# Conditioned residual on one core: loads and stores of the turns cut at other places, and one wait of the store queue taken out

## What is computed

```python
w = weights[conditions]                                # (64, 64, 64) out of (200, 64, 64)
return x + jnp.einsum('bct,bcd->bdt', x, w)            # x is (64, 64, 512)
```

## Time and profile before

| | |
|---|---|
| median of three executions | 46.13 us (45.98 to 49.01) |
| the profiled execution | 45.98 us, span 44.7 us in the trace |
| TensorE busy | 30.7 us, 69% of the span |
| VectorE busy | 15.1 us, 34% |
| ScalarE busy | 13.4 us, 30% |
| DMA | 17.83 MB, 399 GB/s over the span |
| mean granted clock of TensorE | 0.992 of full speed |

### The profile page before, as it was taken

The page is one execution under the profiler, slowest core; times in us unless marked ns, Lnnn a source line. Parts: engine busy times, 40 slices in busy tenths (PEclk is TensorE's granted clock), DMA queues, the critical chain, the costliest instruction groups (busy, mean ns, idle before and its releaser), DMA issues.

```text
span 44.7 us, 329 instructions
## 1 busy us (share of the span) xinstructions
PE 30.7 (69%) x100; PEld 13.2 (29%) x100; DVE 15.1 (34%) x24; ACT 13.4 (30%) x16; POOL 1.6 (4%) x9
## 2 busy tenths in 40 slices
PE   0040000699999679999999799999999999910000
PEld 0040000435334045452543244534445344200000
DVE  1310000000019980957820580094095082073000
ACT  0894000000000072935800580093094080071000
POOL 4009000000000000000000000000000000000000
PEclk9999999999999999999999999999999999999996
DMA  0589999999999999999997988998899999999993
GB/s 0 88 337 403 433 425 411 455 418 418 455 403 447 499 440 469 469 469 469 469 440 315 418 374 374 528 484 352 381 396 425 455 381 403 433 440 396 418 425 139
DMA packets 1586, 17.83 MB, mean 399 GB/s; under 512 B 178, under 2 KB 178, under 8 KB 178
## 3 DMA queue, kind: packets, MB, share of 16 engines
q1 hardware_dynamic: 1440, 16.78, 89.2%
q0 software_dynamic: 144, 1.05, 5.6%
q10 hardware_dynamic: 2, 0.00, 0.0%
HBM read 9.44 MB, written 8.39 MB: 399 GB/s over the span
## 4 chain that ended last, share of the span: by engine, by line
DMA 50%; PE 31%; SPq 4%; DVE 3%; issue 1%; POOLq 0%
DMA x_sb<-x 50%; PE product L166 31%; SPq L94 4%; DVE y_sb L216 3%; POOLq L134 0%
## 5 line engine op out<-in xcount | busy, mean ns | idle before, releaser
L166 PE MATMUL product<-x_sb,w_diag 128*128 (+1 forms) x40 | 17.7, 597 | 0.3 <-POOLq L134 0.3
L216 DVE COPY y_sb<-product 128x1024 f32<-128x1024 f32 x8 | 9.8, 1225 | 12.8 <-PE product L166 10.5
L117 ACT COPY y_sb<-product 128x1024 f32<-128x1024 f32 x8 | 8.1, 1013 | 13.6 <-PE product L166 11.3
L146 PE MATMUL product<-x_sb 128*128 128x512 f32 x10 | 7.0, 872 | 5.3 <-DMA x_sb<-x 5.3
L166 PEld LDWEIGHTS product<-x_sb,w_diag 128*128 128x128 f32 x40 | 7.4, 190 | 10.5 <-issue 10.5
L158 PE MATMUL product<-x_sb,w_all 64*64 64x512 f32 x48 | 5.5, 599 | 0.7 <-DVE w_all L205 0.7
L146 PEld LDWEIGHTS product<-x_sb 128*128 128x128 f32 x10 | 2.8, 288 | 8.8 <-issue 8.8
L111 ACT COPY w_diag<-w_all 64x256 f32<-64x256 f32 x1 | 0.6, 628 | 12.1 <-DVE w_all L205 12.1
L202 DVE TENSOR_TENSOR gathered<-gathered,piece 128x64 f32<-128x64 f32 x1 | 0.3, 270 | 10.1 <-DMA gathered<-weights,table_row 10.1
L158 PEld LDWEIGHTS product<-x_sb,w_all 64*64 64x64 f32 x48 | 2.5, 199 | 3.6 <-issue 2.2
L205 DVE STREAM_TRANSPOSE w_all<-gathered 128x2048 f32<-128x2048 f32 x1 | 2.3, 2312 | 0.0
(11 more groups left out here) (9 smaller groups left out, 1.3 us busy)
## 6 DMA issues: line engine op xcount, KB each, us to landing
x_sb<-x SPq DMA_DIRECT2D x4, 1024.0 KB, 9.1
x_sb<-x SPq DMA_DIRECT2D x1, 4096.0 KB, 22.3
out<-y_sb SPq DMA_DIRECT2D x1, 3072.0 KB, 9.7
out<-y_sb SPq DMA_DIRECT2D x3, 1024.0 KB, 5.0
out<-y_sb SPq DMA_DIRECT2D x1, 2048.0 KB, 6.9
condition<-conditions ACTq DMA_DIRECT2D x1, 0.2 KB
gathered<-weights,table_row POOLq DMA_INDIRECT x1, 9.7
```

The source lines that it names most:

```text
L117: nc.scalar.copy(y_sb[:, 4 * turn:4 * turn + 2, :], product[turn % SETS][0][:, :, :]).then_inc(moved_by_act, 1)
L146: nc.tensor.matmul(product[1][0][:, 0, :], x_sb[:, 0, 0:P], x_sb[:, 0, :], start=True, stop=True)
L166: product_of = nc.tensor.matmul(product[s][j][:, g, :], w_diag[:, s, 2 * j + g, :], x_pair(2 * j + g), start=True, stop=True)
L216: nc.vector.tensor_copy(y_sb[:, 4 * turn + 2:4 * turn + 4, :], product[turn % SETS][1][:, :, :]).then_inc(moved_by_dve, 1)
```

## The change

`LOADS` had one load for turns 4 to 7 (4 MB); now turn 4 is loaded by itself (1 MB) and turns 5 to 7 together (3 MB). `STORES` had turns 0 to 2 in one store (3 MB), turns 3 and 4 in one (2 MB), then single turns; now turns 0 and 1 are one store, turns 2 and 3 one (2 MB each), and turns 4 to 7 are stored singly. The wait ahead of the first store is taken out.

```diff
-    LOADS = [(0, 0), (1, 1), (2, 2), (3, 3), (4, 7)]
-    STORES = [(0, 2), (3, 4), (5, 5), (6, 6), (7, 7)]
+    LOADS = [(0, 0), (1, 1), (2, 2), (3, 3), (4, 4), (5, 7)]
+    STORES = [(0, 1), (2, 3), (4, 4), (5, 5), (6, 6), (7, 7)]
...
-
-            sp.wait_ge(moved_by_dve, SETS + 1)
             for first, last in STORES:
```

## The result

The changed kernel takes 47.10 us (median of 6, 46.75 to 47.17), the kernel before 46.07 us (median of 6). The ratio is **1.022, 95% interval 1.020 to 1.024**: slower by about 1.0 us. The forecast was 46.1, no change, with a range up to 46.7. One of the six executions before, at 49.01 us, fell in a slower state of the chip and is left out of the ratio. The profiled execution took 46.75 us (span 45.4 us), the quickest of its six and 0.77 us more than the profiled one of before, so the trace shows some three quarters of the loss.

What follows compares the result with a forecast made beforehand. The prediction took the DMA engines as the bound: 45.98 us profiled, + 0.1 for packets, - 0.05 for the two starts, gives 46.03; with the median 0.15 above the profiled execution, it forecast 46.1 us, no change, range 45.6 to 46.7.

Steps and rivals of the forecast that it cites:

- The bound: Whole kernel: the DMA engines limit it, at 2.4 to 2.5 us per MB; TensorE's chain is a close second.
- The chain's rival: TensorE's turns 4 to 7: their 0.32 to 0.90 us gain reaches the end, 45.1 to 45.7 us; chance 0.09.
- The wait's removal: Ahead of the first store: alone gives 0; with the new list the store is issued 1.8 us sooner, gaining 0 to 0.05.
- A store that stands in the queue sooner starts no sooner: First store, behind the loads: earlier issue doesn't start its data earlier, as loads last until about 25.1; gain 0 to 0.05 us.
- The signs that I had named: 3 MB load landing after 26, or steps above 2.6 us per MB, would mean reads and writes hinder each other.
- The row I leaned on: Old kernel's 4 MB load: kept 2.42 us per MB with the first store queued for its last 2.36 us.
- The rival of the shared queue: Early store alternates with the 3 MB load, which lands near 29.2, delaying turn 5; 46.6 to 47.4 us; chance 0.08.
- Packets and further transfers: Loads and stores cut into more, smaller transfers: 0.02 to 0.21 us more, taken as 0.1.
- The uncovered part of a transfer: Two further transfers: each shows up to 2.35 us that are not data, giving 47 to 50.7 us; chance 0.03.

Runs made afterwards that it cites:

- multiplied3: The changed kernel with the first store held until TensorE is through with turn 2; 46.82 us, ratio 1.017 to the kernel before.
- hold_landed: The changed kernel with the first store held until the 3 MB load has landed; 47.72 us, ratio 1.040 to the kernel before.

## Why the prediction was wrong

**The bound** was named rightly. The DMA engines set the end, and TensorE's chain does not: TensorE lost its stop before turn 4, its last product came 0.3 us sooner, and the last store, issued at 40.34, took 5.0 us to land in place of 4.0. The forecast had 39.7 to 40.4 and 4.3 to 5.0. The chain's rival is refuted.

**The wait's removal** was right for the old list and wrong in its consequence for the new one. The step that failed is "A store that stands in the queue sooner starts no sooner: the loads ahead of it still last until about 25.1", with its gain of 0 to 0.05 us and no price. The store did start no sooner. But the last of the loads ahead of it landed at 25.88: the store's mere presence slowed them, by 0.73 us per engine in the profiled execution, and the kernel's median rose by about 1.0 us. I bounded that cost only with a row on the order in the queue, and the order was kept. The signs that I had named for reads and writes that hinder each other were a landing after 26 and steps above 2.6 us per MB; the landing stayed just short of its mark, the 2.63 us per MB of that load passed the other.

**The row I leaned on** could not carry it. I took the first store of before as "in the queue for the last 2.36 us of the 4 MB load", which still kept 2.42 us per MB. Of these 2.36 us, 0.85 are the way to the engines and 0.4 the way of the load's last data to its landing: the true overlap was 1.1 us. At that distance there is no loss, and 1.4 us more bring most of it. The row lay on the harmless side of a steep rise, and I read it as if it held for any distance.

**The rival of the shared queue** had the right place (the early store, the 3 MB load) and the wrong mechanism and size. The engines didn't alternate, in one queue or two. It also had 4.1 us of data left at 21.0; counted from the store's arrival at 22.2 to the end of the data, 2.5 were left. The load landed at 25.9, not 29.2, and TensorE never waited for it; its price reached the end directly, as lost time of the bound resource. I had given it 0.08 and thought it harmful only beyond 28.4 us, the point at which turn 5 wants its x. For a queue that is full to the end there is no such point: each us lost anywhere in it is lost at the end.

**Packets and further transfers** were sized well: 0.1 us was the term, and the kernel with the wait back is at 1.002 (0.999 to 1.004), 0.1 us. The uncovered part of a transfer shows only where the queue is empty.

**Open.** Why a store behind a load slows it is not shown. One reading, which no run here tests, is that the store's data are fetched from SBUF ahead of their turn and that this gets in the way of the load's last packets. The stretch also differs between executions of nearly the same order: multiplied3, whose first store went out 0.05 us later, had 0.95 us of it and took 46.97 us in its profiled execution, against 0.73 and 46.75. That may be why the median lost 0.3 us more than the profiled execution, the quickest of the six; the other five were not traced.

## What to carry to other kernels

In a kernel whose DMA queue is full to the end, try not to issue the first store as early as its data allow. Here it had to reach the engines, about 0.9 us after its issue, in about the last 1.1 us of the loads' data: a store held until they had landed left a gap (1.040), one that came 1.9 us or more before their end stretched the load (1.016 to 1.029), and one at 1.5 us cost little (1.005). A wait that looks redundant can be such a timing device once the list beside it changes, so look at what it delays and not only at what it guards. And a busy share near 100% doesn't say that an engine runs at its full rate; divide its busy time by packets of one size.

## What the runs showed of the hardware

- A load with a store issued behind it some 2.5 us or more before its data end lost 0.7 to 1.2 us per engine over its last 45 to 64 KB per engine, with a store of 256 KB (0.70) as of 2 MB (0.73), and in the same queue or another (0.85). With 1.9 us it lost 0.50, with 1.1 us nothing, and nothing with a load behind it (0.913 us for a packet of 24 KB).
- A store whose queue was empty had its first packet 0.8 to 0.9 us after its issue began (hold_landed).
- A 2 MB store on ScalarE's queue, issued at 21.14 us, did not come between the packets of a 3 MB load on SyncE's; its first ones began at about 25.2.
